# Routing weights broadcast by DMA, the masked last key tile left out, first transfers and waits rearranged

## The reference

```python
q, k, v = x @ wq, x @ wk, x @ wv              # 16 query heads, 4 key/value heads of 128
k_ctx, v_ctx = ctx @ wk_ctx, ctx @ wv_ctx
q, k, k_ctx = rms_norm(q), rms_norm(k), rms_norm(k_ctx); q, k = rope(q), rope(k)
k_full, v_full = concat(k_ctx, k), concat(v_ctx, v)      # 4096 + 256 keys
mask = concat(zeros(L, T), where(j > i, -inf, 0))        # causal on the 256 own keys
out = softmax(q @ k_full.T * scale + mask) @ v_full @ wo
...
scores = sigmoid(x @ gate_w); top 6 of 32 experts, normalised -> combine[t, e]
act = silu(x @ wg[e]) * (x @ wu[e])
y = sum_e combine[:, e] * (act @ wd[e]) + shared expert
```

## Time and profile before

| | |
|---|---|
| median of three runs | 1089.95 us |
| the profiled execution | 1091.2 us |
| its span, first to last instruction | 1089.3 us |
| TensorE, matmuls | 1059.5 us busy, 97% |
| TensorE, weight loads | 942.2 us, 87% |
| VectorE | 754.3 us, 69% |
| ScalarE | 556.6 us, 51% |
| GpSimd | 150.7 us, 14% |
| chain that ended last | TensorE 93%, VectorE 3%, DMA 2%, ScalarE 1%, GpSimd 1%, "issue" 1% |

### The profile page before, as it was taken

The page is one execution under the profiler, slowest core; times in us unless marked ns, Lnnn a source line. Parts: engine busy times, 40 slices in busy tenths (PEclk is TensorE's granted clock), DMA queues, the critical chain, the costliest instruction groups (busy, mean ns, idle before and its releaser), DMA issues.

```text
span 1089.3 us, 17054 instructions
## 1 busy us (share of the span) xinstructions
PE 1059.5 (97%) x6701; PEld 942.2 (87%) x6701; DVE 754.3 (69%) x1634; ACT 556.6 (51%) x956; POOL 150.7 (14%) x151
## 2 busy tenths in 40 slices
PE   4999999998999999999999999999999899999998
PEld 3888888886999999999999999999777599999997
DVE  4765777648777777777777777777268677667675
ACT  3443334334765566666556666658035444545442
POOL 2633444330000000000000000003121040000000
PEclk9999999999999999999999999999999899999999
DMA  6468764498004230043101350003530155455540
GB/s 226 161 207 290 251 231 159 141 318 299 3 2 165 64 102 2 1 165 117 49 1 50 119 165 3 1 30 149 221 154 1 59 179 199 175 184 194 179 169 20
DMA packets 63023, 141.66 MB, mean 130 GB/s; under 512 B 3776, under 2 KB 42592, under 8 KB 61536
## 3 DMA queue, kind: packets, MB, share of 16 engines
q1 hardware_dynamic: 62944, 140.58, 37.3%
HBM read 104.36 MB, written 36.18 MB: 129 GB/s over the span
## 4 chain that ended last, share of the span: by engine, by line
PE 93%; DVE 3%; DMA 2%; ACT 1%; POOL 1%; issue 1%; SPq 0%; DVEq 0%
PE bank L423 57%; PE bank L442 16%; PE bank L519 11%; PE bank L574 2%; PE bank L587 1%; PE bank L700 1%; PE bank L452 1%; DMA w_ctx_raw<-in_w_ctx 1%; DMA v_spill<-v_stage 1%; PE bank L647 1%; PE bank L657 1%; PE bank L544 1%; DVE conv_acc L1002 1%; DVE scores L884 0%; PE bank L477 0%
## 5 line engine op out<-in xcount | busy, mean ns | idle before, releaser
L938 DVE TENSOR_TENSOR pT_lo<-bank,pT_hi 128x512 fp32r<-128x512 f32 x272 | 186.0, 689 | 122.7 <-ACT pT_hi L1332 122.5
L423 PE MATMUL bank<-pT_hi,vN 128*128 128x256 f32 x1088 | 244.7, 288 | 0.0
L1332 ACT CAST pT_hi<-bank 128x512 fp32r<-128x512 f32 x272 | 158.6, 587 | 164.4 <-PE bank L519 159.1
L423 PE MATMUL bank<-kT,qT_hi 128*128 128x512 f32 (+1 forms) x576 | 189.4, 410 | 3.4 <-DVE scores L884 3.4
L423 PEld LDWEIGHTS bank<-pT_hi,vN 128*128 128x128 f32 x1088 | 185.7, 188 | 7.1
L884 DVE TENSOR_SCALAR_CACHE_REDUCE scores<-bank 128x512 f32<-128x512 f32 x256 | 169.3, 682 | 1.4 <-DMA v_spill<-v_stage 1.3
L519 PE MATMUL bank<-ident,scores 128*128 128x128 f32 x1088 | 163.2, 272 | 0.9 <-DVE pT_lo L938 0.9
L442 PE MATMUL bank<-w_ctx_hi,ctx_hl 128*128 128x512 f32 x512 | 146.4, 398 | 14.4 <-POOL ctx_hl L1469 8.0
L1303 ACT ACTIVATE scores<-scores,neg_max 128x1024 f32<-128x1024 f32 (+1 forms) x128 | 154.9, 1210 | 5.7 <-DVE neg_max L895 5.7
L423 PE MATMUL bank<-fT_hi,e_hl 128*128 128x256 f32 x816 | 155.9, 284 | 0.0
L423 PE MATMUL bank<-pT_lo,vN 128*128 128x256 f32 x544 | 153.2, 282 | 0.0
(11 more groups left out here) (203 smaller groups left out, 1364.7 us busy)
## 6 DMA issues: line engine op xcount, KB each, us to landing
e_raw<-in_experts SPq DMA_DIRECT2D x51, 768.0 KB, 4.3
k_spill<-k_stage SPq DMA_DIRECT2D x16, 1024.0 KB, 4.5
v_spill<-v_stage SPq DMA_DIRECT2D x16, 1024.0 KB, 8.1
vN<-v_spill SPq DMA_DIRECT2D x16, 1024.0 KB, 5.2
kT<-k_spill SPq DMA_DIRECT2D x15, 1024.0 KB, 5.5
ctx_raw<-in_ctx SPq DMA_DIRECT2D x15, 512.0 KB, 3.9
w_raw<-in_w_qkv SPq DMA_DIRECT2D x6, 1024.0 KB, 5.4
wo_sb<-in_wo SPq DMA_DIRECT2D x4, 1024.0 KB, 9.1
```

What stands on the lines that cost most here:

```text
L423: done = e.matmul(dst, lhs(a), rhs(w), start=first and m == 0, stop=last and m == 2)
L938: e.tensor_tensor(ring[1][:, :], bank[tb][:, :], ring[0][:, :], ALU.subtract).then_inc(p_lo, 1)
L1332: e.copy(ring[0][:, :], bank[tb][:, :]).then_inc(p_hi, 1)
```

## The change

On SyncE, the routing weights are written to memory once (`c_spill`) and read back by eight DMAs, each of which writes four experts' rows into all 128 partitions; GpSimd's broadcasts and their buffers are gone. In attention, `keys_of` and `seen` leave the last key tile out for query tile 0: scores, eviction and exponential of 128 keys fewer, one transpose fewer in the last pair, three matmuls with v over half of the queries. At the start ctx batches 1 and 2 and the first w_raw are issued ahead of rope and the norm weights, `split_w(0)` moves from tile 0 to tile 1 on ScalarE and VectorE, and GpSimd's `rope_tables` move from tiles 0 and 1 to tiles 1 and 2. The evictions of head 1 wait for less, query tile by query tile. The last down tile counts each half, so each output addition has its own wait.

```diff
+def keys_of(qt, c):
+    if c < NCHK - 1:
+        return CH
+    return L if qt else P
+def seen(kt, qt):
+    return qt == 1 or kt < KTILES - 1
...
 def score(s):
-                n = CH if c < NCHK - 1 else L
+                n = keys_of(qt, c)
...
 def turn_weights(h, kk):
+                    if not seen(kt, qt):
+                        continue
...
 def weigh(n):
-                for i, kt in enumerate((2 * kk, 2 * kk + 1)):
-                    done = three(bank[5 + z][:, 0:L], lambda v: vN[:, v, kt, :], lambda p: ring[p][:, i * L:(i + 1) * L],
-                                 kt == 0, kt == KTILES - 1)
+                order = (1, 0) if kk == NPAIR - 1 else (0, 1)
+                for i in order:
+                    kt = 2 * kk + i
+                    q0 = 0 if seen(kt, 0) else P
+                    done = three(bank[5 + z][:, q0:L], lambda v: vN[:, v, kt, :], lambda p: ring[p][:, i * L + q0:(i + 1) * L],
+                                 kt == 0, kt == KTILES - 2)
...
 def down(j):
+                    if j == NFT - 1:
+                        done.then_inc(last_down, 1)
-                done.then_inc(downed, 1)
+                if j < NFT - 1:
+                    done.then_inc(downed, 1)
...
 # VectorE and ScalarE, ctx stage
-                if i == 0:
+                if i == 1:
                     split_w(0)
...
 def evict(s):
                 if h == 1:
-                    for slot in range(2):
-                        dve.wait_ge(k_out[slot], 16 * NBATCH // 2)
-                        dve.wait_ge(v_out[slot], 16 * NBATCH // 2)
                     dve.wait_ge(k_turned, NT)
-                    dve.wait_ge(k_tail, 1)
+                    dve.wait_ge(k_out[0], 16 * NBATCH // 2)
+                    if qt:
+                        dve.wait_ge(k_out[1], 16 * NBATCH // 2)
+                        dve.wait_ge(v_out[0], 16 * NBATCH // 2)
+                        dve.wait_ge(k_tail, 1)
...
 def weigh_up(j):
-                dve.wait_ge(comb_done, ex1 // 4 + 1)
+                dve.wait_ge(comb_in[ex0 // 4], comb_total + 16)
+                dve.wait_ge(comb_in[ex1 // 4], comb_total + 16)
...
 # VectorE, end
-            dve.wait_ge(downed, NFT)
             for tt in range(TT):
+                dve.wait_ge(last_down, tt + 1)
                 e.tensor_tensor(fn[:, tt, :], x_sb[:, tt, :], bank[4 + tt][:, :], ALU.add).then_inc(o_done, 1)
...
 # GpSimd
-            e.memset(causal[:, 2 * P:], MASKED).then_inc(consts, 1)
...
-                if i < 2:
-                    rope_tables(i)
+                if 1 <= i < 3:
+                    rope_tables(i - 1)
...
-            for q in range(NE // 4):
-                pool.wait_ge(flat_in[q % 2], 16 * (q // 2 + 1))
-                e.partition_broadcast(comb[:, 4 * q:4 * q + 4, :].rearrange("p e t -> p (e t)"), flat_c[q % 2][0:1, :]).then_inc(comb_done, 1)
...
 # SyncE
             e.dma_start(x_sb[:, :, :], t["x"]).then_inc(x_in, 16)
+            load_ctx(1)
+            load_w(0)
+            load_ctx(2)
             e.dma_start(rope_raw[:, :, :, :], t["rope"]).then_inc(sides_in, 16)
             e.dma_start(w_norm[:, 0, :], t["q_norm_w"].partition_broadcast(P)).then_inc(sides_in, 16)
             e.dma_start(w_norm[:, 1, :], t["k_norm_w"].partition_broadcast(P)).then_inc(sides_in, 16)
             e.dma_start(k_w[:, :], t["k_norm_w"].rearrange("(p a) -> p a", a=1)).then_inc(sides_in, 16)
-            load_w(0)
-            for b in range(1, NCR):
-                load_ctx(b)
...
+            def broadcast_weights():
+                sp.wait_ge(topk, 19)
+                e.dma_start(c_spill, cT[:, :]).then_inc(c_out, 16)
+                sp.wait_ge(c_out, 16)
+                for q in range(NE // 4):
+                    e.dma_start(comb[:, 4 * q:4 * q + 4, :].rearrange("p e t -> p (e t)"),
+                                c_spill[4 * q:4 * q + 4, :].rearrange("e t -> (e t)").partition_broadcast(P)).then_inc(comb_in[q], 16)
...
                 if j == 0:
-                    fetch_weights(0)
-                    fetch_weights(1)
-                if j < NE // 4:
-                    fetch_weights(j + 2)
+                    broadcast_weights()
```

More of the change, by code:

```diff
@@ L200, in build_program @@
         v_spill = nc.dram_tensor("v_spill", (NKV, 2, P, KTILES, HD), F32).ap()
+        c_spill = nc.dram_tensor("c_spill", (NE, L), F32).ap()
         keep = region["keep"]
@@ L206, in build_program @@
         upto = keep.take("upto", [P])
-        causal = keep.take("causal", [3 * P])
+        causal = keep.take("causal", [2 * P])
         power = keep.take("power", [P])
@@ L320, in build_program @@
         fT_hl = [over_gate.take("fT_hi", [KD, L], F32R), over_gate.take("fT_lo", [KD, L], F32R)]
-        over_yT = Region(nc, m23.base, 8192)
-        flat_c = [over_yT.take(f"flat_c{i}", [4 * L], parts=1) for i in range(2)]
         comb = region["s01"].again().take("comb", [NE, L])
@@ L346, in build_program @@
         self_out = sem("out_self")
-        k_in, v_in = [sem(f"in_k{i}") for i in range(NPIECE)], [sem(f"in_v{i}") for i in range(NPIECE)]
+        k_in, v_in = [sem(f"in_k{i}_then_comb") for i in range(NPIECE)], [sem(f"in_v{i}_then_comb") for i in range(NPIECE)]
         small_in, w_xb_in = sem("in_small"), sem("in_w_xb")
         w_xa_in, w_z_in, w_out_in = sem("in_w_xa"), sem("in_w_z"), sem("in_w_out")
-        e_in, flat_in = ctx_in + first_in, [sem(f"in_flat{i}") for i in range(2)]
+        e_in, c_out = ctx_in + first_in, sem("out_c")
+        comb_in, comb_total = (k_in + v_in)[:NE // 4], 16 * NKV
         ctx_total = [16 * (NBATCH // NCR)] * NCR + [16] * BT
@@ L374, in build_program @@
         fT_h, fT_l, rl_ct, sg_done, sent, topk = (sem(n) for n in ("fT_h", "fT_l", "rl_ct", "sg_done", "sent", "topk"))
-        e_hi, e_lo, upped, silu, up_weighted, prod, act_hi, act_lo, downed, comb_done, o_done = (
-            sem(n) for n in ("e_hi", "e_lo", "upped", "silu", "weighted", "prod", "act_hi", "act_lo", "downed", "comb_done", "o_done"))
+        e_hi, e_lo, upped, silu, up_weighted, prod, act_hi, act_lo, downed, last_down, o_done = (
+            sem(n) for n in ("e_hi", "e_lo", "upped", "silu", "weighted", "prod", "act_hi", "act_lo", "downed", "last_down", "o_done"))
         def own_index(n):
@@ L482, in pe_program @@
                 if i == 1:
-                    pe.wait_ge(consts, 8)
+                    pe.wait_ge(consts, 7)
                     for tt in range(TT):
@@ L886, in evict @@
                 else:
-                    e.tensor_tensor_reduce(out=s_buf[row][:, lo:lo + L], in0=bank[b][:, 0:L], in1=causal[:, (1 - qt) * P:(3 - qt) * P], scale=1.0,
+                    n = keys_of(qt, c)
+                    e.tensor_tensor_reduce(out=s_buf[row][:, lo:lo + n], in0=bank[b][:, 0:n], in1=causal[:, (1 - qt) * P:(1 - qt) * P + n], scale=1.0,
                                            scalar=MASKED, op0=ALU.add, op1=ALU.max, accum_out=chunk_max[row][:, c:c + 1]).then_inc(maxed, 1)
@@ L1459, in pool_program @@
                             channel_multiplier=1).then_inc(consts, 1)
-            pool.wait_ge(consts, 8)
+            pool.wait_ge(consts, 7)
             def inverse_std(n, tt):
@@ L1673, in load_e @@
                     e.dma_start(e_raw[j % NRAW][:, :, :], t["experts"][j]).then_inc(e_in[j % NRAW], 16)
-            def fetch_weights(q):
-                if q < NE // 4:
-                    sp.wait_ge(topk, 19)
-                    if q >= 2:
-                        sp.wait_ge(comb_done, q - 1)
-                    e.dma_start(flat_c[q % 2][0:1, :].rearrange("o (e t) -> o e t", e=4), cT[4 * q:4 * q + 4, :]).then_inc(flat_in[q % 2], 16)
+            def broadcast_weights():
[5 more added lines that the diff above has]
+                                c_spill[4 * q:4 * q + 4, :].rearrange("e t -> (e t)").partition_broadcast(P)).then_inc(comb_in[q], 16)
             for j in range(NRAW):
```

4 lines of the change are left out of this document (2 added, 2 removed).

## The result

The kernel after takes 1078.58 us (median of four runs, 1077.7 to 1079.19), the kernel before 1089.78 in the same comparison: ratio 0.989, 95% interval 0.988 to 0.990. The profiled execution took 1078.46 us; its span is 1076.5, 12.8 less than before.

A forecast was written before the change was run, and what follows sets the result against it. TensorE, busy 97% of the span, was taken to bound the kernel. Start +0.3, seam -1.3, attention -2.4 and tail -0.6 sum to -4.0 us, giving 1085.9 from the median 1089.95; range 1079.5 to 1088.5, by its working 1084.5 to 1087.5.

The forecast's parts named there:

- Routing weights: Expert routing: removing GpSimd's eight partition broadcasts gains 0, since TensorE has no gap while they run.
- Start, the stall: Start: GpSimd's 12.21 us idle before its first affine_select stays; dropping the memset ahead gains 0, at most 0.2.
- Rival A: Start: half of GpSimd's idle time before affine_select goes, gain 6.2 us more, 1079.7; chance 0.10.
- Start, the moved steps: Start: moved rope tables gain 0.36 us, moved weight split makes TensorE wait some 0.65; net loss 0.3.
- Transfers at the start: Start: ctx batches and first w_raw issued ahead of rope and norm weights; 0, with 1 us of loss as bound.
- Seam: Between heads 0 and 1: evictions no longer wait for the last v_spill; gain 1.3 us, bounds 0.5 and 1.4.
- Attention: Sixteen heads, masked key tile left out: 1.8 us from transposes plus 0.6 from narrow matmuls, gain 2.4.
- rival C: Attention: narrow matmuls follow their columns, saving 5.7 us instead of 0.6; a head shorter by 0.47; 1080.8; chance 0.10.
- Routing's new transfers: Expert stage: eight DMA broadcasts ahead of tile 8, which lands at 889.8 with 6.4 us to spare; cost 0.
- B: Expert stage: DMA broadcasts crawl and tile 8 comes late; 1099.6 at 129 GB/s, 1109 at 103 GB/s; chance 0.10.
- Tail: After the last matmuls: a count per half lets the first addition run under them; gain 0.6 us, bounds 0.4 and 0.7.
- rival D: Moved waits come back: start loses 1.5, seam gives 0.5, tail 0.4; sum -1.8, 1088.1; chance 0.08.

The follow-up runs named there:

- e3: Kernel after plus one 8-element partition broadcast, read by nobody, as GpSimd's very last operation: 1087.10 us, ratio 0.997 to the kernel before.
- f3: Kernel of e3 with GpSimd's low half of ctx tile 0 moved ahead of its three affine_selects: 1084.81 us, ratio 0.995 to the kernel before.
- i1: Kernel of e3 without any affine_select, identity made by transfers through memory, causal mask and part of the ranking left out: 1087.22 us, a single execution.
- e2: Kernel after with the old routing restored (SyncE flattens the weights, eight GpSimd partition broadcasts): 1086.69 us, ratio 0.9965 to the kernel before.
- f1: Kernel after with the split of the first w_raw and the rope tables both moved back to their old places: 1080.68 us, ratio 0.991 to the kernel before.
- e1: Kernel before with only the routing weights sent through memory, no GpSimd partition broadcast left: 1085.53 us, ratio 0.995.
- f2: Kernel after with the start transfers in the old order, rope and norm weights first: 1078.69 us, ratio 0.989 to the kernel before.
- g1: Kernel after plus eight more 512 KB transfers, written to memory, queued ahead of expert tile 8: 1088.82 us, ratio 0.999 to the kernel before.
- h1: Kernel of e2 with VectorE writing the low half of ctx tile 0 and GpSimd taking tile 1 before its affine_selects: 1078.86 us, ratio 0.989 to the kernel before.
- e4: Kernel before with only the masked last key tile left out for query tile 0: 1088.23 us, ratio 0.997.
- e5: Kernel of e3 with one 8-element affine_select added behind the small broadcast: 1085.42 us, ratio 0.9955 to the kernel before.
- f5: Kernel after with only the split of the first w_raw moved back to tile 0: 1078.59 us, ratio 0.989 to the kernel before.

## Why the prediction was wrong, and where it was right

- **Routing weights**: the broadcasts "are off the path: TensorE has no gap while they run [...], so their going gains 0". This is the step that failed. The sentence is true of the place where the broadcasts run and false of the kernel: an operation can cost time where it does not stand. e3 shows it with a broadcast that does next to nothing.
- **Start, the stall**: 12.21 us of idle time, "so nothing that the profile shows". It stood on the engine for which TensorE waited in its largest gap, and the sum carried it over unexplained. Rival A had the effect and 0.10, priced with half of the stall gone. All of it went, and 7.59 us of TensorE's gap with it, so even A's 1079.7 was too high. The argument against A (the wait stands before affine_select, which stays) is what f3 and i1 refute: the place of the stall says nothing about its owner.
- **Start, the moved steps**: +0.3 for a wait of 0.65 less a gap of 0.36. The wait came, 0.67 in after and 0.69 in e2; where the stall is kept, e2, the x projection is 0.58 later than before, near the forecast. But beside the vanished stall the same edit is worth 2.5 us (f1), since an earlier TensorE meets rope tables that were nearly on time for a later one. Routing alone gives 4.7 us and the rest alone 3.6; together it is 11.2. The 3 us above their sum fit these moved steps, which gain 2.5 without the stall and lose 0.6 with it: the gap of 2.05 in e1, and the low clock behind it.
- **Transfers at the start**: 0 forecast; f2 shows none.
- **Seam**: -1.3 forecast, -1.43 in the trace. No other wait took its place.
- **Attention**: -2.4 forecast, -2.62. A head takes 0.164 less (forecast 0.15), where rival C wanted 0.47. If the 16 transposes went at 0.11, the 96 narrow matmuls saved 0.009 each, not 0.059: the row of the 128-column full-float matmul was the right neighbour.
- **Routing's new transfers**: 0, as forecast, with tile 8 at 878.8. In the coordinates of before that is 891.2 against my 889.8, so the reckoning was 1.4 us too early and the spare 5 us instead of 6.4. B's last figure, 1109, is about a microsecond too high by its own working.
- **Tail**: -0.6 forecast, -0.67. In the timeline after, one addition runs under the last three matmuls and one behind them, where both stood behind before:

```profile
1068.94 4.34 PE L434 MATMUL bank<-e_hl,act 128*128 128x512 f32 x18
...
1072.63 1.38 DVE L1222 TENSOR_TENSOR fn<-x_sb,bank 128x512 f32<-128x512 f32 x2 [1.50 <-PE bank L434]
```

- **The rest**, +0.38, -0.89 and +0.26 in three stretches for which the sum had no term. The state-space stretch, which no edit touches, took 104.0 to 105.4 us in these kernels, in no order that follows an edit; where the granted clock falls in it differs from kernel to kernel. From the x projection to the scores it takes either 208.5 or 208.9, and both values occur with the start of after (g1 and after). I count this as the scatter of one profiled run against another.
- **The range**: its working gave 1084.5 to 1087.5 with start, seam and tail at their bounds. The upper end is added up wrong: these three alone give the 1088.1 of rival D, and with the narrow matmuls 1088.7. This did not decide anything, as the time came out on the other side.

So the terms for seam, attention and tail stand, and the zeros for the transfers; the total was wrong by one mechanism and by what it did to its neighbour.

## What to carry to other kernels

Idle time that ends in "issue" early on an engine that others wait for may have an owner elsewhere; before pricing its removal at zero, look for operations of a special kind anywhere in that engine's program, and test with one tiny operation added or removed. If such an operation has to stay, put nothing urgent behind its stall: giving another engine the first step was worth as much as removing it, within the noise (h1). The releaser that the view names can mislead: for the same stall it says "issue" in before, and a cast of ScalarE in e4, where the select needs none, and in f3, where it had been done for 6 us. And when one edit moves the start of the critical engine by microseconds, price all other edits again against the new arrival times: what was a gap of 0.36 became one of 2.1.

## What the runs showed of the hardware that I had not expected

- A single GpSimd partition broadcast, even as the last operation of the program, brings 11.1 to 12.3 us of idle time behind the first memsets of GpSimd. All eight kernels with one show it in their traces (before, e2, e3, e4, e5, f3, h1, i1), and none of the six without (0.24 us). Before the broadcast itself stands only a wait for its input (5.96 us in e3, ended by ScalarE). The Trainium skill (GPSIMD Engine Reference, section 2.1 Instruction dispatch) gives about 6 us for the first call to a freshly loaded kernel. If this is the same thing, it is twice as long here, and it does not stand at the call.
- After a gap of some 2 us TensorE's granted clock sometimes goes to the lower of its levels (1.2 GHz) for 2 to 4 us and sometimes does not: behind the same gap of 2.1 us at the end of the ctx stage it read 1.00 in before, after and f5, but 0.85 and 0.72 in the two stretches of 4 us from 240 on in f2, and 0.76 and 0.82 in those from 248 on in e2. From the scores to the turned weights f2 and e2 took 22.1 and 22.4 us, against 20.9 in after. A removed gap can thus be worth nearly twice its length (e1: 2.05 of gap, and 12 matmuls in 4 us instead of 20, some 1.6 us more).
- Eight transfers that each read 4 KB of memory for all 128 partitions ran at 338 to 428 GB/s with the DMA engines full, in the end as fast as the expert loads behind them (427 and 412 from 879 to 883). The ones written to memory came to 317 by the delay of tile 8, and to 340 in the view.
